# A fused attention and ternary feed-forward layer: the levels' transposition on SyncE, the norms' columns on GpSimd, squares on ScalarE

## The reference

```python
def _layernorm(x, axis=-1, eps=1e-05):
    ...
    return (x - m) / jnp.sqrt(v + eps)

x = x + _layernorm(attn(_layernorm(x)))
x = x + _layernorm(ffn(_layernorm(x)))
```

## Time and profile before

| | us |
|---|---|
| median of 3 runs | 1174.39 |
| lowest, highest | 1171.98, 1174.90 |
| the profiled execution | 1171.96 |
| its span in the trace | 1170.3 |

### The profile page before, as it was taken

How to read it: one execution, slowest core, us unless ns; L and a number is a source line. 1 busy time by engine, 2 the same in 40 slices (tenths; PEclk the granted TensorE clock), 3 DMA queues, 4 the chain that set the end, 5 groups by cost and what they waited for, 6 DMA issues and landing times.

```text
span 1170.3 us, 44847 instructions
## 1 busy us (share of the span) xinstructions
PE 1095.2 (94%) x18656; PEld 732.9 (63%) x18656; DVE 988.7 (84%) x2562; ACT 707.8 (60%) x1493; POOL 588.0 (50%) x715
## 2 busy tenths in 40 slices
PE   4899999999999999999999999999999999998652
PEld 3566666676666666766666666666666676665321
DVE  5748998889988888899988888898888889987574
ACT  5445666766666667666666666656666666565432
POOL 2334555555555555555545555555555565454411
PEclk9989999999999999999999999999999999999765
DMA  9746667755657676656566676556667665554231
GB/s 272 159 87 139 140 155 160 163 138 139 139 119 138 155 164 164 139 132 136 127 139 153 165 159 138 127 123 139 151 152 165 148 151 133 116 113 120 65 64 47
DMA packets 204831, 161.81 MB, mean 138 GB/s; under 512 B 150448, under 2 KB 150704, under 8 KB 204528
## 3 DMA queue, kind: packets, MB, share of 16 engines
q1 hardware_dynamic: 199888, 141.86, 55.7%
q0 software_dynamic: 4736, 17.04, 4.1%
HBM read 40.87 MB, written 16.78 MB: 49 GB/s over the span
## 4 chain that ended last, share of the span: by engine, by line
PE 72%; DVE 18%; issue 4%; DMA 3%; SPq 2%; ACT 1%; POOLq 1%; POOL 0%; DVEq 0%; ACTq 0%
PE f_job L1356 46%; PE f_st L1457 5%; PE f_o L1474 5%; PE f_o L1479 4%; PE f_job L1533 3%; PE f_job L1432 2%; PE f_job L1515 2%; DVE f_stage L955 2%; DVE f_bst L1001 2%; DVE f_rmax L969 2%; PE f_job L1523 1%; DVE f_inverse L993 1%; DVE f_x L1045 1%; DVE f_o L991 1%; PE f_job L1440 1%
## 5 line engine op out<-in xcount | busy, mean ns | idle before, releaser
L488 POOL TENSOR_SCALAR_AFFINE_SELECT f_PT<-f_PT 64x512 f32<-64x512 f32 (+1 forms) x256 | 203.4, 812 | 157.6 <-ACT f_PT L654 107.5
L503 POOL TENSOR_TENSOR f_square<-f_stage 128x512 bf16<-128x512 f16 x128 | 131.1, 1047 | 92.1 <-ACT f_stage L632 79.3
L494 POOL TENSOR_TENSOR f_OTl<-f_o,f_OTh 128x256 f16<-128x256 f32 x127 | 84.6, 673 | 140.0 <-ACT f_OTh L672 140.0
L1356 PE MATMUL f_job<-f_xTh,f_wqh 128*128 128x256 f16 x512 | 140.8, 275 | 14.9 <-DMA f_xTl<-f_xl 14.8
L632 ACT ACTIVATE f_stage<-f_job,f_bias 128x256 f16<-128x256 f32 x256 | 106.6, 468 | 75.9 <-PE f_job L1356 68.7
L1356 PE MATMUL f_job<-f_xTh,f_wql 128*128 128x256 f16 x512 | 140.2, 274 | 0.0
L1356 PE MATMUL f_job<-f_xTl,f_wqh 128*128 128x256 f16 x512 | 140.1, 274 | 0.0
L1356 PE MATMUL f_job<-f_xTh,f_wkl 128*128 128x256 f16 x512 | 139.7, 273 | 0.0
L1356 PE MATMUL f_job<-f_xTh,f_wkh 128*128 128x256 f16 x512 | 139.7, 273 | 0.0
L1356 PE MATMUL f_job<-f_xTl,f_wkh 128*128 128x256 f16 x512 | 139.7, 273 | 0.0
L955 DVE SCALAR_TENSOR_TENSOR f_stage<-f_job,f_bias,f_stage 128x256 f16<-128x256 f32 x256 | 110.9, 475 | 32.7 <-ACT f_stage L632 32.7
(11 more groups left out here) (197 smaller groups left out, 2975.9 us busy)
## 6 DMA issues: line engine op xcount, KB each, us to landing
f_stacks<-f_stage SPq DMA_DIRECT2D x380, 128.0 KB
f_xin<-x SPq DMA_DIRECT2D x32, 512.0 KB, 6.2
f_x<-x SPq DMA_DIRECT2D x32, 512.0 KB, 4.5
out<-f_z POOLq DMA_DIRECT2D x31, 512.0 KB, 3.5
f_Vmix<-f_V SPq DMA_DIRECT2D x32, 256.0 KB, 6.2
f_Vmix<-f_V SPq DMA_DIRECT2D x64, 128.0 KB, 6.3
f_stacks<-rows_const SPq DMA_DIRECT2D x3, 512.0 KB, 4.9
f_stacks<-wqT SPq DMA_DIRECT2D x2, 512.0 KB, 5.8
```

The source lines that it names most:

```text
L488: nc.gpsimd.affine_select(out=d, in_=d, compare_op=ALU.is_ge, fill=0.0, base=odd * SUB, pattern=[[0, 4], [0, TP], [1, SUB]], channel_multi ...
L494: nc.gpsimd.tensor_tensor(OT[s % 2][1][:, g, :], o32[:, g % 2, :], OT[s % 2][0][:, g, :], ALU.subtract).then_inc(OTl_made, 1)
L503: nc.gpsimd.tensor_tensor(square[:, 2 * m + pair, :], h, h, ALU.mult).then_inc(squared, 1)
L1356: mm = pe.matmul(dst, lhs[a](c), rhs[b](c), start=(n == 0), stop=(n == 3 * KC - 1))
```

## The change

The arithmetic is the same apart from the second variance. The parts:

- Levels. `level` writes to a buffer of its own, `q16` (before it shared `x2h`). For the steps 0 to 28 (`by_queue` is 29) SP turns it with one DMA for each tile (`turn_levels`) straight into `qT`, and PE waits for that in `second`; `turn_q` on PE and `keep_q` on ACT remain for the last three steps. `turn_x2` moves from the end of a step to the start of the next.
- Second variance. `x_stats` on DVE is gone. ACT sums the squares of the 511 columns after the first of the Hadamard product (`square_sum`) before it rounds; the first column, which holds the mean, is left out of the scale and of the levels, so its correction is gone too.
- Columns. Adding epsilon, the signed products and the differences of the three normalisations, each on 128 x 2 elements, go from DVE to POOL (`front_columns`, `y_columns`, `z_level`, `z_columns`).
- The squares for `norms` go from four instructions on POOL to two of twice the length on ACT.
- `keys(s, 2, 0)` and `keys(s, 2, 1)` stand together, before `weigh(s, 0)`.
- The orders of SP, POOL, ACT and DVE in the loop are written anew; `norm_z` and `finish_out` of a step come in the step after.

The diff, cut to its core:

```diff
+            def turn_levels(k, t):
+
+                sp.wait_ge(q_made, TP * k + t + 1)
+                until(sp, f_product, TP * (k - 1) + t + 1)
+                sp.dma_start(qT[:, t], q16[:, t, :], transpose=True).then_inc(q_moved[t], 16)
...
             for s in range(STEPS - 1):
                 n, m, k = s + 1, s + 2, s - 1
+                if s:
+                    mix_values(s)
+                if has(k - 1):
+                    turn_x2(k - 1, 0)
+                    turn_x2(k - 1, 1)
                 max_rows(s)
+                if has(k):
+                    load_res(k)
+                restack_high(n)
+                if has(k - 1):
+                    turn_levels(k - 1, 0)
+                restack_low(n, (0, 1))
+                if has(k - 1):
+                    turn_levels(k - 1, 1)
+                restack_low(n, (2, 3))
                 if s < 2:
                     load_rows(n)
-                if has(k):
-                    load_res(k)
+                if has(m):
+                    turn_x(m)
                 if has(m + 1):
                     load_front(m + 1)
-                if s:
-                    mix_values(s)
-                restack_high(n)
-                restack_low(n, range(4))
-                if has(m):
-                    turn_x(m)
-                if has(k):
-                    turn_x2(k, 0)
-                    turn_x2(k, 1)
-
+
+            turn_x2(last - 2, 0)
+            turn_x2(last - 2, 1)
...
+            def front_columns(m):
+
+                pool.wait_ge(f_stats_made, TP * m + TP)
+                until(pool, xn_made, TP * m)
+                nc.gpsimd.tensor_scalar(f_veps, f_mv[:, m, :, 1], EPS, None, ALU.add).then_inc(f_veps_made, 1)
+                nc.gpsimd.tensor_scalar(f_off, f_mv[:, m, :, 0], -1.0, None, ALU.mult).then_inc(f_turned_sign, 1)
...
+            def y_columns(k):
+
+                pool.wait_ge(y_stats_made, TP * k + TP)
+                until(pool, x1_made, TP * k)
+                nc.gpsimd.tensor_scalar(y_veps, y_mv[:, :, 1], EPS, None, ALU.add).then_inc(y_veps_made, 1)
+                nc.gpsimd.tensor_scalar(y_off[:, k, :], y_mv[:, :, 0], -1.0, None, ALU.mult).then_inc(y_turned_sign, 1)
...
+            def z_level(k):
+
+                pool.wait_ge(qinv_made, TP * k + TP)
+                pool.wait_ge(x_squared, TP * k + TP)
...
                 n, m, k = s + 1, s + 2, s - 1
-                square_of(n, 0)
+                if has(m):
+                    front_columns(m)
+                if has(k - 2):
+                    finish_out(k - 2)
                 if s and has(k):
                     heads_low(k, 2)
                 if has(k):
                     heads_low(k, 3)
-                if has(m):
-                    front_root(m)
-                if has(n):
-                    square_of(n, 1)
                 if has(s):
                     clear_future(s, 0)
+                if has(k - 1):
+                    z_level(k - 1)
+                if has(s):
                     clear_future(s, 1)
                 if has(k):
-                    y_root(k)
+                    y_columns(k)
                 if has(s):
+                    heads_low(s, 0)
                     clear_future(s, 2)
                 if has(k - 1):
-                    z_root(k - 1)
+                    z_columns(k - 1)
                 if has(s):
-                    heads_low(s, 0)
                     clear_future(s, 3)
                     heads_low(s, 1)
-                if has(k - 1):
-                    finish_out(k - 1)
...
+            def square_of(n, m):
+
+                act.wait_ge(qk_high, 8 * n + 8)
+                until(act, norms_product, n)
+                nc.scalar.activation(square[:, 2 * m:2 * m + 2, :].rearrange("p a (g n) -> p a g n", g=2),
+                                     stage[:, 2 * m, :, :].rearrange("p (a g) n -> p a g n", a=2),
+                                     ACT.Square).then_inc(squared, 1)
...
+            def square_sum(k, t):
+
+                act.wait_ge(qinv_made, TP * k + t + 1)
+                nc.scalar.activation(unread[:, t, 1:D], bank("h", t)[:, 1:D], ACT.Square,
+                                     accum_out=x_ss[:, k, t:t + 1]).then_inc(x_squared, 1)
+
             def round_levels(k, t):
-                act.wait_ge(qinv_made, TP * k + t + 1)
-                nc.scalar.activation(bank("h", t)[:], bank("h", t)[:], ACT.Identity, bias=round_col[:],
+                act.wait_ge(x_squared, TP * k + t + 1)
...
+                qk_high_part(n, 0)
                 if has(k):
                     invert(k, 3)
-                qk_high_part(n, 0)
                 if s:
                     heads_high(k, 2)
                 qk_high_part(n, 1)
+                if has(k - 2):
+                    norm_z(k - 2)
                 keep_max(s)
                 qk_high_part(n, 2)
+                if has(m):
+                    front_norm(m, 0)
                 if has(k):
                     heads_high(k, 3)
                 if has(k - 1):
+                    square_sum(k - 1, 0)
                     round_levels(k - 1, 0)
+                if has(m):
+                    front_norm(m, 1)
                 qk_high_part(n, 3)
                 exps(s, 0, 0)
+                exps(s, 0, 1)
                 if has(k - 1):
                     level(k - 1, 0)
-                exps(s, 0, 1)
...
+                invert(s, 0)
+                exps(s, 2, 0)
+                square_of(n, 0)
+                exps(s, 2, 1)
...
-            def x_stats(k):
-                dve.wait_ge(x1_made, TP * k + TP)
...
                 dve.wait_ge(h_product, TP * k + t + 1)
-                dve.wait_ge(x_stats_made, TP * k + t + 1)
-                sums = bank("h", t)[:, 0:1]
-                note(nc.vector.scalar_tensor_tensor(sums, x_mv[:, k, t, 0:1], -D * SX, sums, ALU.mult, ALU.add))
-                settled()
-                note(nc.vector.tensor_reduce(a, bank("h", t)[:], AX_X, ALU.max, apply_absolute_value=True))
+                note(nc.vector.tensor_reduce(a, bank("h", t)[:, 1:D], AX_X, ALU.max, apply_absolute_value=True))
                 settled()
                 note(nc.vector.tensor_scalar(q, a, 1e-5, 1.0 / QMAX, ALU.max, ALU.mult))
                 settled()
+                until(dve, qsquare_made, k)
...
                 qk_low_part(n, 0)
-                if has(k):
-                    normalise(k, 3)
                 qk_low_part(n, 1)
                 if s == 0:
                     keep_norms(0)
-                if has(m):
-                    front_stats(m)
+                if has(k):
+                    normalise(k, 3)
                 if has(k - 1):
                     find_scale(k - 1, 0)
+                qk_low_part(n, 2)
+                if s < 4:
+                    weight_guard(s)
+                if has(k - 1):
+                    find_scale(k - 1, 1)
+                qk_low_part(n, 3)
+                if has(m):
+                    front_low(m)
                 if s == 0:
                     fold_bias()
-                qk_low_part(n, 2)
-                if has(m):
-                    front_offset(m)
-                if s < 4:
-                    weight_guard(s)
-                qk_low_part(n, 3)
-                if has(k - 1):
-                    find_scale(k - 1, 1)
                 if has(k):
                     y_out(k, 0)
-                if has(m):
-                    front_low(m)
-                if has(k):
                     y_out(k, 1)
                     y_stats(k)
                 normalise(s, 0)
+                if has(k - 1):
+                    scale_out(k - 1, 0)
                 if has(k):
                     residual(k)
                     fold(k, 0)
                     fold(k, 1)
-                    fold_again(k, 0)
                 if has(k - 1):
-                    scale_out(k - 1, 0)
                     scale_out(k - 1, 1)
+                maxima(n, 0)
+                if has(k - 1):
                     z_stats(k - 1)
                 if has(k):
+                    fold_again(k, 0)
                     fold_again(k, 1)
-                maxima(n, 0)
+                maxima(n, 1)
                 keep_norms(n)
-                maxima(n, 1)
                 normalise(s, 1)
+                maxima(n, 2)
+                if has(m + 1):
+                    front_stats(m + 1)
                 if has(k):
                     x2_low(k, 0)
-                maxima(n, 2)
-                if has(k - 1):
-                    z_columns(k - 1)
+                normalise(s, 2)
                 maxima(n, 3)
+                split_max(n)
                 if has(k):
                     x2_low(k, 1)
-                split_max(n)
-                if has(k):
-                    x_stats(k)
-                normalise(s, 2)
...
                     out_product(k, 0)
-                if has(k - 1):
-                    turn_q(k - 1, 0)
                 keys(s, 1, 0)
```

(3 more changed lines are left out.)

252 lines of the change are left out of this document (133 added, 119 removed).

## The result

| | before | after |
|---|---|---|
| median, us | 1173.39 (4 runs) | 1194.11 (4 runs) |
| lowest to highest | 1171.98 to 1174.90 | 1193.48 to 1197.67 |
| span of the profiled execution | 1170.3 | 1191.4 |

The changed kernel is slower: the ratio is 1.0185, 95% interval 1.017 to 1.0199. The forecast was 1157, with a range to 1172.

A forecast was written before the change was run, and what follows sets the result against it. PE's own instructions were taken to bound the kernel from 60 to 1090 us. Savings of 13.3 (turnings) and 3.5 (keys), 16.8 us if nothing waits, gave 1157.6 in runs; forecast 1157, own range 1151 to 1163, wider range 1150 to 1172.

The forecast's parts named there:

- What leaves PE: PE's own work: both turn_q gone in 29 of 32 steps, 13.3 us, plus third keys 3.5; sum 16.8, 0.56 a step.
- the keys: Third keys' halves together on PE: 0.10 to 0.12 us saved in each of 31 turns, say 3.5 us.
- The turned levels (delivery 3): SP's transpositions for the ternary product: some 1.5 us free at the median; low parts queued behind reached 2.5 us later.
- The rival that named it: Levels land late, or the low parts behind them: 0.7 us a step, 20 us, 1177; chance 0.05.
- DVE shut out: POOL blocks DVE's residual and butterflies, 0.46 us each; with five, +24 us, 1199; chance 0.09.
- the turning of the maxima: PE's turn of the maxima, after DVE's work: 3.0 us free before, 1.1 or some 0.7 left after.
- Head and tail: Start and end of the run: both set to 0, with 3 us either way.
- Maxima's rows late (0.20): Rows landing late at the first keys: PE waits 0.3 to 0.6 us in 29 steps, around 1169; chance 0.20.
- POOL's column operations: Twelve more a step on POOL, those without a root taken as 0.3 us each.

The follow-up runs named there:

- base B: The changed kernel with stand-ins as base A, but each tile's levels moved in one copy instead of two; 1180.86 us, ratio 1.0074.
- stand-ins: Plain copies of the same bytes replacing each DMA transposition, so nothing is turned; the kernel before edited so took 1173.38 us, ratio 1.0003.
- base A: The changed kernel with two plain copies in place of each DMA transposition, the levels' too; 1197.89 us, ratio 1.019.
- the gated kernel: Base B with GpSimd waiting for VectorE's residual before it starts heads_low and the third group's clearing; 1183.12 us, ratio 1.007.

## Why the prediction was wrong

- **What leaves PE: right.** 18.9 us of busy time, against 16.8. In mid-run a step of PE without its waits went from 33.50 to 32.98 us (32.82, and the 0.16 of "issue" ahead of the first ternary product, which was not a wait for anyone), 0.52 against the 0.56 forecast. Of this the keys are 0.15, where I had 0.10 to 0.12, though alone they gained nothing (1.0011), for f_stage came late instead.
- **The turned levels (delivery 3): the levels right, what queues behind them wrong.** This is the step that failed. The levels themselves cost 1.9 us in three waits, as the slack of 1.5 had said. Of the low parts I wrote that SP reaches them 2.5 us later, "but the loads of x and the copies of V are out of the way". Those loads stood ahead of the high pieces, where SP waited for ACT in any case. SP's waits of the kernel before, 60 to 1090 us:

```profile
SPq L373 <- ACT f_stage L632: 40.3, 28, 2.1
```

  Taking them out only lengthens that wait, and the same list after has 76.1 us for L396. Nothing of the 3.26 us was given back. The slack to spend was 5.22 - 1.98 = 3.2 in the mean (1.4 in the one step that I had read). Counted from the scores before them, the scores were due 0.4 earlier (28.27 us instead of 28.67), and the high pieces left 0.1 later. So 3.8 was asked of 3.2 in the mean; the waits are larger, 0.90 a step, and I take that from the spread, since a step with time to spare gives none of it to the next. I never subtracted the one from the other. The rival that named it got 0.05 and 0.7 a step; its price was 24.9 us at the scores, and base B gave 14 to 17 us back for one issue less a tile.
- **DVE shut out: the mechanism right, its place and weight wrong.** The price was named as 0.46 an instruction, and it is 0.46 to 0.48 (0.87 to 0.89 for 0.41). It falls on residual and butterflies in every step, not in a few. I forecast the harm at the turning of the maxima; it came at the bank of `values(n, 1)`, which I had not followed. It counts for 1.3 us of waiting in the changed kernel, and for 13.4 once the first layer is off. That DVE "held its pace" in mid-run belonged to the order of that kernel, and the change moved it: the clearing began 1.95 us behind the residual in that step before (668.22 against 666.27), and 1.23 in the step of base B above, with `heads_low` ahead of it. The moment alone does not decide: in the kernel before with the keys together it began 1.72 behind, and the butterflies kept 0.42.
- **Head and tail: set to 0 within 3, and too low.** Together they are 7.1 of the 21.1 us: 3.5 up to the fourth call of `norms` and 3.6 behind the last. Moving `load_rows` cost 6.8 in base B. What makes the tail longer was not tried.
- **Maxima's rows late (0.20): did not happen.** Their landing fell from a median of 3.0 to 1.9 us, since fewer loads run beside them, and PE waited 0.6 in all.
- **POOL's column operations: fair.** Those without a root take 0.19 to 0.27 (the first of a chain 0.49), against 0.3.

The sum with stand-ins: 1197.9, less 17.0 for an issue a tile, less 6.8 for the rows, less 13.4 for the clearing, makes 1160.7, if these add (they were not run together); the forecast in the same terms is 1173.4 - 16.8 = 1156.6. The 4 us between are no more than the uncertainty of base A. In base B 2.2 us of waits at the scores are left, and behind the last `norms` it takes 101.2 us, where the kernel before with stand-ins takes 96.4.

Open: what decides between POOL and DVE when both come. In the kernel before, the clearing of mid-run came amid the butterflies and waited; in the gated kernel `heads_low` came amid them and got in. Open too: why the same issue holds the queue for 1.25 us in one step and over 2 in another. Turning the levels from another queue was not tried.

## What to carry to other kernels

When a DMA is put into an in-order queue, add its issue time to everything behind it and subtract that from the slack of the last instruction there that is needed, counted from its issue to its use less its landing; what is taken out ahead of an earlier wait of that queue gives nothing back. When a kernel with one engine at 99.9% is changed in many places, its list of waits shows only the first layer of the loss: take that one away and read the list again before counting a gain. A duration measured beside another engine belongs to that order of arrival, and has to be priced anew when either engine's order moves.

## What was not expected of the hardware

- One issue of a transposition of 128 x 512 elements held SP's queue for some 1.25 us in most cases and 2.0 to 2.9 in the others, 1.49 and 1.84 in the mean for the two of a step. That is not a matter of transposing: two plain copies of the same bytes took 1.33 to 1.35 in most steps of base A and up to 2.87 in the others, and gave the same time in the whole kernel (1.0003 before, 1.019 against 1.0185 after). The low pieces have such long issues as well. Of some 220 from 130 to 1060 us, each usually 0.6, over 0.9 took 21 in the kernel before, 6 in the changed one and 27 in base B, whose level copies all took 0.65. So an issue's mean has to be taken with its neighbours in the queue.
- Between POOL and DVE the first to come does not keep the port for its run: in the gated kernel each butterfly beside `heads_low` and the two clearings took 0.87 to 0.89 us, three in a row, where 0.41 is its time alone, although DVE had been running without a gap. The Trainium skill, SBUF — State Buffer (the section on its two sides), says that the pair of ports is held for one whole instruction, and the engine that comes second blocks; alternation by instructions agrees with that. It does not say who is next when both wait.
- A clearing cut from 512 columns to 64 still takes 0.39 to 0.65 us, yet the butterflies beside it take 0.44 in the mean. So an instruction's duration on POOL, which the profile shows only roughly, does not tell what DVE pays for it; why was not tried.
